# Image 0's chain packed into the dense expert layer, and its second expert layer begun inside image 1's choice of experts

## The reference, cut to what matters

```python
x = x + _L0_conv_ref(_ln_c(x), ...)            # window attention
t = _to_tokens(x); t = t + _L0_ffn_ref(_ln_t(t), ...)   # 8 experts, top 2, out = tokens + sum
x = x + _L1_conv_ref(_ln_c(x), ...)            # conv1, group norm, taps, group norm, relu, conv2, group norm, relu, + input
t = _to_tokens(x); t = t + _L1_ffn_ref(_ln_t(t), ...)   # 16 experts, top 2: silu(x w1) * (x w2), then w3
```

## Time and profile before

| | us |
|---|---|
| median of 3 runs | 718.04 |
| lowest and highest | 716.93, 719.39 |
| the profiled execution, its own time | 720.16 |
| its span in the trace | 718.3 |

### The profile page before, as it was taken

The page is one execution under the profiler, slowest core; times in us unless marked ns, Lnnn a source line. Parts: engine busy times, 40 slices in busy tenths (PEclk is TensorE's granted clock), DMA queues, the critical chain, the costliest instruction groups (busy, mean ns, idle before and its releaser), DMA issues.

```text
span 718.3 us, 16000 instructions
## 1 busy us (share of the span) xinstructions
PE 563.4 (78%) x5352; PEld 467.6 (65%) x5353; DVE 357.8 (50%) x1040; ACT 355.7 (50%) x843; POOL 423.9 (59%) x484
## 2 busy tenths in 40 slices
PE   2677788868599999999996689836269999999900
PEld 2565677657377776677774468515169999999900
DVE  6977778646600611210024454582756555555523
ACT  4476687975573536641144522224036665666600
POOL 1677798765774786753343000077567777777771
PEclk9999999899997999999995597855569999999965
DMA  9452222111364452322580000011223332333536
GB/s 298 147 143 78 82 75 83 51 52 49 128 218 162 156 187 106 111 110 85 185 249 0 1 0 1 0 48 50 67 60 107 100 96 86 108 97 96 198 113 212
DMA packets 59039, 75.30 MB, mean 105 GB/s; under 512 B 9470, under 2 KB 49366, under 8 KB 58302
## 3 DMA queue, kind: packets, MB, share of 16 engines
q1 hardware_dynamic: 51614, 60.49, 27.1%
q0 software_dynamic: 5632, 11.62, 4.8%
q10 hardware_dynamic: 1728, 2.36, 0.9%
HBM read 57.96 MB, written 23.81 MB: 114 GB/s over the span
## 4 chain that ended last, share of the span: by engine, by line
PE 60%; DVE 13%; POOL 8%; ACT 8%; issue 7%; DMA 3%; SPq 1%; POOLq 0%; DVEq 0%; ACTq 0%
PE bank L800 13%; PE bank L762 9%; PE bank L861 8%; PE bank L745 8%; PE bank L811 7%; PE bank L722 3%; PE bank L316 3%; ACT normed L906 3%; POOL gathered_or_att L570 2%; POOL padded_or_w L561 2%; POOL returned L640 2%; PE bank L791 2%; PE bank L760 1%; POOL gathered_or_att L579 1%; DVE ln_stats L1092 1%
## 5 line engine op out<-in xcount | busy, mean ns | idle before, releaser
L605 POOL TENSOR_TENSOR padded_or_w<-padded_or_w,gathered_or_att 128x384 f32<-128x384 f32 x96 | 95.5, 1001 | 74.9 <-ACT padded_or_w L980 71.2
L621 POOL DMA_INDIRECT sorted_x<-normed,slot x72 | 71.3, 990 | 101.6 <-DVE slot L1323 80.4
L640 POOL DMA_INDIRECT returned<-gathered_or_att,home_of_slot x104 | 102.7, 988 | 31.7 <-issue 22.6
L980 ACT ACTIVATE padded_or_w<-bank,moe_b 128x384 f32<-128x384 f32 x96 | 55.4, 579 | 101.0 <-PE bank L745 100.7
L762 PEld LDWEIGHTS bank<-moe_or_conv,padded_or_w 128*128 128x128 f32 x576 | 82.0, 200 | 31.3 <-issue 10.4
L762 PE MATMUL bank<-moe_or_conv,padded_or_w 128*128 128x128 f32 x576 | 85.2, 287 | 0.0
L745 PE MATMUL bank<-chan_major,moe_or_conv 128*128 128x384 f32 x192 | 82.5, 516 | 0.0
L1352 DVE TENSOR_TENSOR att_or_moe<-att_or_moe,bank 128x256 f32<-128x256 f32 x104 | 43.7, 420 | 50.2 <-PE bank L811 26.8
L994 ACT ACTIVATE att_or_moe<-bank 128x256 f32<-128x256 f32 x104 | 39.9, 383 | 57.0 <-PE bank L800 56.5
L660 PE MATMUL bank<-padded_or_w 64*64 64x64 f32 x1152 | 48.1, 235 | 25.3 <-issue 17.0
L660 PEld LDWEIGHTS bank<-padded_or_w 64*64 64x64 f32 x1152 | 42.0, 147 | 34.9 <-issue 34.9
(11 more groups left out here) (179 smaller groups left out, 1092.3 us busy)
## 6 DMA issues: line engine op xcount, KB each, us to landing
gathered_or_att<-combine SPq DMA_DIRECT2D x24, 768.0 KB, 4.2
padded_or_w<-windows SPq DMA_DIRECT2D x192, 48.0 KB, 1.9
sorted_x<-in_pad_rows SPq DMA_DIRECT2D x26, 260.0 KB, 7.2
padded_or_w<-sorted_x SPq DMA_DIRECT2D x26, 260.0 KB
padded_or_w<-in_moe_w SPq DMA_DIRECT2D x8, 512.0 KB, 5.3
qy<-returned SPq DMA_DIRECT2D x6, 384.0 KB, 4.8
out<-residual ACTq DMA_DIRECT2D x12, 192.0 KB, 2.1
normed<-returned SPq DMA_DIRECT2D x6, 384.0 KB, 5.4
```

Source lines behind the costliest of these rows:

```text
L605: nc.gpsimd.tensor_tensor(HB[n % DRING], HB[n % DRING], GB_[k % 3][:, n % 4, :], ALU.mult).then_inc(S("gated"), 1)
L621: nc.gpsimd.indirect_dma_start(xs_dram[b], bass.IndirectOffsetOnAxis(ap=POS[b][:, k, t:t + 1], axis=0), TNR[b][:, t, :], None).then_inc(S( ...
L640: nc.gpsimd.indirect_dma_start(yt_dram[b], bass.IndirectOffsetOnAxis(ap=HOMES[b][:, j:j + 1], axis=0), YR[k * RING + j % RING], None).then ...
L980: nc.scalar.activation(HB[n % DRING], banks[HBANK[n % 2]][:, 0:DG], ACT.Gelu, bias=B1C[:, e:e + 1]).then_inc(S("gelu"), 1)
```

## The change

1. `order`: image 0's whole chain, through its `RC` piece 1, now stands inside the second half of `D`. The taps come six pieces to a step, over three steps. `XL` 0's tiles 0, 2 and 4 are normalized by DVE, as in the other layer norms.
2. Inside `D` the reciprocal square roots of image 0 (`XL` 0, `LR` 1 0 and its three group norms) are made by POOL with a power of -0.5 (`PW`, `PG`). Image 1's group norms use four Newton steps on DVE (`newton`). ACT's square root stays for `XL` 1 and `LR` 1 1.
3. After `D`, image 1's chain stands alone, except for pieces 2 to 4 of image 0's choice, its prefix sums, its slots and its scatter, which stand around `XC` 1 and the taps.
4. The table of tiles and experts, until now the end of `slots`, is a piece of its own (`RJ`) behind the scatter.
5. The second expert layer of image 0 is written out tile by tile (`MT`, `tile_steps`), with its expert numbers taken from a register by shifts as before. Tiles 0 to 12 stand between pieces 2, 3 and 4 of image 1's choice, the others behind image 1's slots. Image 1's layer stays a loop.
6. Banks: transposes and outputs of the tiles share banks 2 and 3, hidden values take 6 and 7; with that come new waits between PE and ACT, and ACT scales tile j-4 before it applies silu to tile j-2. Image 1's prefix sums go to banks 4 and 5, its conv2 has two banks and not four.

```diff
-            (52, ("SQ", "XL", 0)), (52, ("LV", "XL", 0)), *every(53, 1, groups("LT", "XL", 0)), *every(54, 1, groups("XG", 0)),
+            (52, ("PW", "XL", 0)), (52, ("LV", "XL", 0)), *every(53, .5, groups("LT", "XL", 0)), *every(54, .5, groups("XG", 0)),
...
+        order += [*groups("XUH", 1), *groups("XZ", 1), *normed("LR", 1, 1), *groups("RT", 1, 1), ("LG", 1, 1), ("RC", 1, 1, 0), ("RE", 1, 1), *choice(1, 1, 1, 2),
+                  *tiles(0, 3), ("RC", 1, 1, 2), *tiles(3, 6), ("RC", 1, 1, 3), *tiles(6, 10), ("RC", 1, 1, 4), *tiles(10, 13)]
+        order += [("RP", 1), ("RS", 1), ("RJ", 1), *tiles(MID_TILES, J + 4), ("M", 1), *[("F", b) for b in range(NB)]]
...
-        UP = ((6, 7), (4, 5, 3, 2))
+        UP = ((6, 7), (4, 5))
         HBANK, YBANK = (2, 3), (4, 5)
+        PREFIX = ((6, 7), (4, 5))
+        HID_BANK, ROW_BANK = (6, 7), (2, 3)
...
+                nc.gpsimd.tensor_tensor(lv[:, 5, :], lv[:, 3, :], EXPO[:, 0:1].broadcast_to([P, TT]), ALU.pow).then_inc(S("ln_root"), 1)
...
+                nc.gpsimd.tensor_tensor(gv[:, 9:10], gv[:, 5:6], EXPO[:, 0:1], ALU.pow).then_inc(S("gn_root"), 1)
...
             run(A=lambda n: attend(att, n), ...
+                MT=lambda t: send_back(0, t - 4), M=lambda b: [send_back(b, j) for j in range(J)])
...
+                    if not isinstance(j, int) or j >= 6:
+                        pe.wait_ge(S("y_ready"), j - 5 + b * J)
...
                     act.wait_ge(S("x_transposed"), j + 1 + b * J)
+                    if j >= 4:
+                        act.wait_ge(S("y_full1"), j - 3 + b * J)
...
                         xt(j, j % RING)
+                    if j >= 4:
+                        tail(j - 4, j % RING)
                     if 0 <= j - 2 < J:
                         nonlin(j - 2, (j - 2) % RING)
-                    if j >= 4:
-                        tail(j - 4, j % RING)
...
+            def newton(gv):
+                v, y, t = gv[:, 5:6], gv[:, 9:10], gv[:, 6:7]
+                link(ts(v, v, 1e-5, None, ALU.add))
+                link(ts(y.bitcast(i32), v.bitcast(i32), 1, None, ALU.logical_shift_right))
+                link(ts(y.bitcast(i32), y.bitcast(i32), -1.0, float(0x5f3759df), ALU.mult, ALU.add))
+                for _ in range(4):
+                    link(nc.vector.scalar_tensor_tensor(t, y, y, v, ALU.mult, ALU.mult))
+                    link(ts(t, t, -0.5, 1.5, ALU.mult, ALU.add))
+                    link(tt(y, y, t, ALU.mult))
```

More of the change, by code:

```diff
@@ L214, in beside, with tiles @@
                 yield from marks.get(n, ())
+        def tiles(first, last):
+            return [("MT", t) for t in range(first, last)]
         half, shared = DN // 2, NB * STEPS
@@ new lines, in metaformer_program @@
+            *every(57, 2, groups("AN", "XL", 0)), (58, ("XC", 0)), (59, ("XCE", 0)), (59, ("GN", "XC", 0)), (61, ("GS", "XC", 0)), (62, ("PG", "XC", 0)),
+            (64, ("XCH", 0)), *every(65, 1 / 6, taps(0, 0, 54)), (68, ("GN", "XM", 0)), (70, ("GS", "XM", 0)), (71, ("PG", "XM", 0)), (73, ("XMH", 0)),
+            *every(74, 1 / 3, [("XU", 0, n) for n in range(8)]), (77, ("GN", "XU", 0)), (80, ("GS", "XU", 0)), (81, ("PG", "XU", 0)),
+            *every(83, .5, groups("XUH", 0)), *every(84, .5, groups("XZ", 0)), (89, ("LN", "LR", 1, 0)), (90, ("PW", "LR", 1, 0)),
@@ new lines, in metaformer_program @@
+            (90, ("LV", "LR", 1, 0)), *every(92, .5, groups("LT", "LR", 1, 0)), *every(93, .5, groups("RT", 1, 0)), (96, ("LG", 1, 0)),
+            (97, ("RC", 1, 0, 0)), (97, ("RE", 1, 0)), (98, ("RC", 1, 0, 1))])
+        order += [*normed("XL", 1), *groups("XG", 1), ("RC", 1, 0, 2), ("XC", 1), ("XCE", 1), ("RC", 1, 0, 3), ("RC", 1, 0, 4), ("RP", 0),
+                  ("GN", "XC", 1), ("GS", "XC", 1), ("XCH", 1), *groups("AN", "XL", 1), ("RS", 0), *taps(1, 0, 54), ("RJ", 0),
+                  ("GN", "XM", 1), ("GS", "XM", 1), ("XMH", 1), *[("XU", 1, n) for n in range(8)],
+                  ("GN", "XU", 1), ("GS", "XU", 1)]
@@ L248, in metaformer_program, with n_of_root @@
         gns = [ph[1:] for ph in order if ph[0] == "GN"]
+        def n_of_root(ph):
+            return [g for g in gns if g[1] == 0].index(ph)
         normed_by = {"LNA": ("LNA",), "XG": ("XL",), "RT": ("LR",)}
@@ L384, in tile_groups, with tile_steps, at, load @@
             group(n, n % 2, None, last=True)
+        def tile_steps(eng, step):
+            E, words, top = EX[1], EPK[0], 2 ** (BITS * RING) - 1
+            word = {}
+            def at(t):
+                q, r = divmod(t, RING)
+                if r == 0:
+                    word["before"] = word.get("now")
+                def load():
+                    if q < J // RING:
+                        word["now"] = eng.value_load(words[0:1, ds(q, 1)], min_val=0, max_val=top)
+                def expert(k):
+                    bits = word["now"] if r >= k else word["before"]
+                    shift = BITS * ((r - k) % RING)
+                    return (bits >> shift) & (E - 1) if shift else bits & (E - 1)
+                step(t, r, q % 2, expert, load)
+            return at
         @block.sync
```

121 lines of the change are left out of this document (74 added, 47 removed).

## The result

The changed kernel takes 732.5 us (median of four executions, 725.9 to 738.3) where the kernel before took 717.5 in the same comparison (four, 714.7 to 719.4): a ratio of 1.0164 with an interval of 1.0117 to 1.0211. It is slower, by 15 us in the medians and by 1.6% in the ratio, and lies outside the predicted range. Medians take all executions, while ratios leave out slow ones, more than 1.5% above the fastest of their kernel, and the profiled execution (738.3, span 736.5) is one of those.

What follows compares the result with a forecast made beforehand. POOL's queue was taken as the bound from the second scatter on; its start moved +9.2 + 1.0 - 19.8 + 1.3 + 15.5 = +7.2, sends -11.6, net -4.4, giving 713.6 us, range 706 to 723.

Steps and rivals of the forecast that it cites:

- the end by its formula: End of the span: second scatter's start + 47.2 + (sends behind it - 1) x 1.293 + 15.4 us.
- The choice with its tiles: Image 1's choice with thirteen tiles in it, up to the second scatter: 31.2 us, or +15.5; bounds 27 and 40.
- the third rival: Thirteen tiles at half clock hold up image 1's choice; scatter 10 to 15 us later, time 724 to 728; chance 0.16.
- the fourth: Rival: new waits in image 0's tiles make PE the bound, above 1.77 us a step; 737 us at 2.0; chance 0.06.
- the dense layer's second half: Dense layer with image 0's chain packed in: ends 9.2 us later (11.3 - 6.1 + 4.0), bounds 5 and 16.
- the added work: On PE in the dense half: conv2 pieces 2.8, transposes 4.0, logits 4.5, sum 11.3 us.
- The removed losses: In the dense half: PE's waits of 1.7 and 1.5 and low clock of 2.9 go, sum 6.1 us.
- the clock: PE's clock in the dense half: 2.9 us of low clock removed, 2.0 behind logits and 1.5 at conv2 added.
- The 2.0 behind the logits: Three dense steps behind image 0's logits run at half speed, costing 3 x 0.66 = 2.0 us.
- The 1.5 at conv2: Conv2's pieces in the dense half may drop the clock; half of 2.9 taken, so 1.5 us.
- the first rival: Packed dense layer keeps its clock, which falls only where PE stands still; time 706 to 710 us; chance 0.18.
- the stretch behind the taps: From image 1's taps to its last group norm: two Newton roots +4.6, image 0's slots gone -3.3, sum +1.3 us.

Runs made afterwards that it cites:

- the two mended kernels: Changed kernel with ACT's layer-norm and group-norm roots, four banks, logits behind the dense layer, conv2 over 128 rows: 706.4 us with thirteen tile steps ahead, 700.3 with none.

## Why the prediction was wrong

**What held.** POOL as the bound, the end by its formula, nine sends ahead, the taps (29.6, forecast 29.5), the way to the taps (23.9, forecast 23.6). The choice with its tiles took 32.4 where 31.2 was forecast, so the third rival is not what made it slower; nor is the fourth, since ACT's last tile starts at 706.3 and POOL's last send at 721.0.

**The step that failed is the dense layer's second half**, +9.2 with bounds of 5 and 16, measured +25.4. Of its three parts the added work was right (11.3; 10.2). The removed losses were not removed: "the wait of 1.7 ... and of 1.5 ..., both behind a change of ACT's table for a square root, which POOL's power makes needless". The power takes 3.2 us, and it stands ahead of DVE and PE just as ACT's change of table did. So PE's waits rose by 5.6 in place of falling by 2.7: the one for the normalized tiles went from 1.67 to 3.48, the second power brought one of 2.09, conv2 has 0.88 and 0.58 where it had 1.55, and image 0's taps have 1.95 where they had none. Putting the layer norms' square roots back took 3.8 us of the waits, and 5.6 off the half with the clock behind them. The wait ahead of the taps stayed (1.97): the forecast had 0.5 for all hand-offs. Whether it comes from the tight packing of group norm and taps or from POOL's power between them stays open, since no run spreads them again or takes image 0's group-norm powers back. Here the prediction costed the power at nothing, with 1.3 as upper end, from rows of other POOL operations; nothing in the trace before was near it, and the cover it named ("PE has dense steps to do meanwhile") is not there: when the power starts, at 283.52, PE has multiplications up to 285.12, and the tiles come at 288.61. Two of the prediction's own signs of being wrong came true, the layer's end past 400 (412.6) and a power of several us.

The second failed part is the clock: +0.6 forecast, +8.7 measured. By the stretches above it costs 0.08 x 20.3 = 1.6 behind the wait of 3.48, 0.04 x 42.1 = 1.7 behind that of 1.95, 0.28 x 18.0 = 5.0 behind conv2 and 0.17 x 20.3 = 3.5 in the last steps. The 2.0 behind the logits was about right: 0.39 x 3.6 = 1.4, and moving the logits out took 6.0 off the last steps, 4.5 of them the logits themselves. The 1.5 at conv2 was 5.1: 18.0 against 12.9 with 128 rows; with 32 packed rows the clock fell there in six profiles of seven. The rest of the last steps' loss stands behind the second power's wait, and the forecast, which had no such waits, had no clock behind them.

The rule on the clock that the first rival rested on (the Trainium skill, "TensorE: Matmul & The Clock Gate", section "HAM oscillation — how this bites in real kernels") puts a fall down to gaps in which PE is idle. Behind the wait of 3.48 the trace agrees. Behind conv2 it does not: with 128 rows and a wait of 0.98 us in the same place the clock held, with 32 rows and waits of 0.88 and 0.58 it fell for some 10 us.

**The second, smaller miss** is the stretch behind the taps, +1.3 forecast, +4.4 measured. Two banks in place of four under conv2 were not costed at all; they are 2.3 of the 3.1. The Newton roots were sized nearly right (2.3 each forecast, 2.5 measured).

**No tiles ahead would have been the better half of the change.** The forecast had them at +15.5 - 11.6 = +3.9; the runs show 4.7 by the trace and 6 between the two mended kernels. That the packed half is worth having was right as well: mended, without the logits' 4.5, it takes 114.0, 7.7 us more than the 106.3 before, and it buys the 20 us of the taps. The forecast for this was 9.2 - 4.5 - 2.0 = 2.7; most of the difference is PE's standing still, 5.1 us there, where the forecast's terms leave 3.7 - 2.7 = 1.0.

**What stays open** is what exactly drops the clock at conv2. It held in all four profiles with 128 rows. With 32 rows packed three to a step it fell in six of seven; with 32 rows one to a step it held in both profiles in mid-layer and fell in the kernel before, where the pieces stand behind a wait of 1.55. With 128 rows behind that same wait (1.64 in the experiment) it held. So neither a wait of that size nor few rows is enough by itself; few rows with a wait nearby mostly are. Packed pieces of 32 rows without any wait were not tried, nor waits of this size ahead of few rows in another place.

## What to carry to other kernels

An operation moved to another engine to spare a stall must be priced on that engine before it counts as a saving; where no row has it, the range must admit that it is longer than what it replaces, and the work queued behind it counts too. A matmul over few rows, amid full ones, can be given zero weights for the other rows at no cost in columns, and here that kept the granted clock at 1.00 in four profiles of four. Work pulled ahead of a queue that is the bound pays only if an item costs less there than in the queue: here thirteen steps cost 16.3 us to spare nine sends of 1.29.

## What the runs showed of the hardware

- A power on POOL takes 3.24 us over 18 columns and 0.56 over one, so 0.16 more for each column, while a product with a constant over 18 columns takes 0.30. The Trainium skill, "GPSIMD Engine Reference", section "2.1 Instruction dispatch", says that such an operation runs as a software loop over the elements; the growth with the columns agrees, and the page has no figure for a power.
- The same matmuls at the same number of columns held the clock with 128 rows (four profiles of four) and mostly lost it with 32 (six of the seven with packed pieces); in the kernel before, too, 0.61 became 1.00. Why is not shown.
- Over all profiles, in the dense layer's second half, the clock fell behind each of the eight waits of PE of 3.11 to 3.49 us, behind five of the six of 2.09 and nine of the twelve of 1.95 to 1.97; behind waits of 0.98 to 1.67 ahead of matmuls over 128 rows it held each time.
- Small DVE operations on two tensors take longer beside a POOL operation: the group norm's L1397 took 0.92 us at 305.19 in the kernel before, beside a gate product, and 0.16 at 404.60 with POOL idle; the layer norm's L1185 took 0.97 and 0.18 above.
- The same code ahead of the change runs at either level: the first steps of the first dense layer took 12.5 us at a clock of 1.00 in the profile with ACT's group-norm roots and 15.7 at 0.79 in the changed kernel's.
